# A one-core perceiver layer: where the first eight attention steps do their splits, loads and seeding

## What is computed

```python
def xattn(inputs_q, inputs_kv, Wq, Wk, Wv, Wo):        # H, HD = 16, 128
    q = (inputs_q @ Wq).reshape(b, sq, H, HD) * (1.0 / np.sqrt(HD))
    k = (inputs_kv @ Wk).reshape(b, skv, H, HD)
    v = (inputs_kv @ Wv).reshape(b, skv, H, HD)
    attn = softmax(einsum('bqhd,bkhd->bhqk', q, k), axis=-1)
    return einsum('bhqk,bkhd->bqhd', attn, v).reshape(b, sq, H * HD) @ Wo

x = x + xattn(layernorm(x), ctx, Wq, Wk, Wv, Wo)       # 1 x 128 x 512 against 1 x 12544 x 512
x = x + decayed_linear_attention(layernorm(x), ...)    # 16 heads of 32
x = x + bitlinear_ffn(layernorm(x), ...)               # 512 -> 2048 -> 512
```

## Time and profile before

| | |
|---|---|
| median of 3 runs | 2038.02 us (2037.34 to 2038.19) |
| the profiled execution: its own time | 2039.78 us |
| its span | 2037.9 us |
| PE busy | 1955.8 us (96%) |
| DVE busy | 1606.4 us (79%) |
| ACT busy | 1127.4 us (55%) |

### The profile page before, as it was taken

How to read it: one execution, slowest core, us unless ns; L and a number is a source line. 1 busy time by engine, 2 the same in 40 slices (tenths; PEclk the granted TensorE clock), 3 DMA queues, 4 the chain that set the end, 5 groups by cost and what they waited for, 6 DMA issues and landing times.

```text
span 2037.9 us, 46247 instructions
## 1 busy us (share of the span) xinstructions
PE 1955.8 (96%) x17334; PEld 1596.3 (78%) x17334; DVE 1606.4 (79%) x3444; ACT 1127.4 (55%) x2484; POOL 272.4 (13%) x465
## 2 busy tenths in 40 slices
PE   5799999999999999999999999999999999999786
PEld 5577887887887987977978978878878878878462
DVE  4788788788888888888888888888888887877426
ACT  3556566666656555555555565555565556555212
POOL 1011111111111111111111111111111111100001
PEclk8899999999999999999999999999999999999888
DMA  5568887887886888787787887888978877765540
GB/s 147 148 113 163 164 162 153 160 165 153 163 161 133 143 161 162 145 160 156 146 165 156 147 156 156 147 155 162 168 147 157 147 136 142 138 121 128 206 177 6
DMA packets 966945, 304.44 MB, mean 149 GB/s; under 512 B 893985, under 2 KB 952865, under 8 KB 965825
## 3 DMA queue, kind: packets, MB, share of 16 engines
q1 hardware_dynamic: 966720, 301.47, 74.8%
HBM read 72.16 MB, written 4.46 MB: 38 GB/s over the span
## 4 chain that ended last, share of the span: by engine, by line
PE 91%; DVE 5%; DMA 2%; issue 1%; ACT 1%; POOL 0%; DVEq 0%; ACTq 0%; SPq 0%; POOLq 0%
PE ps_v L1211 25%; PE ps_s L1196 24%; PE ps_t L1196 19%; PE ps_w L1211 18%; DMA bulk<-in_vo 1%; PE ps_w L1170 1%; DVE pp L875 1%; PE ps_v L1183 1%; PE ps_t L1290 1%; DVE acc L884 0%; PE ps_s L1333 0%; PE ps_v L1297 0%; DVE prob L870 0%; ACT bulk L602 0%; PE ps_s L1152 0%
## 5 line engine op out<-in xcount | busy, mean ns | idle before, releaser
L1196 PE MATMUL ps_s<-bulk 128*128 128x128 f16 (+2 forms) x4752 | 583.4, 272 | 2.7 <-DVE bulk L811 2.7
L1211 PE MATMUL ps_v<-nring,pt 128*128 128x256 f16 x4704 | 581.4, 273 | 3.0 <-DVE acc L884 1.5
L1211 PEld LDWEIGHTS ps_v<-nring,pt 128*128 128x128 f16 x4704 | 458.8, 98 | 63.7 <-DVE acc L794 2.6
L1196 PEld LDWEIGHTS ps_s<-bulk 128*128 128x128 f16 x4752 | 404.6, 98 | 114.7 <-DVE bulk L811 2.9
L1196 PE MATMUL ps_t<-bulk 128*128 128x384 f16 (+2 forms) x3564 | 454.0, 272 | 18.9 <-ACT ps_t L653 17.2
L1211 PE MATMUL ps_w<-nring,pt 128*128 128x256 f16 x3528 | 451.8, 273 | 8.0 <-DVE ps_w L894 6.4
L875 DVE SCALAR_TENSOR_TENSOR pp<-prob,pp 128x384 f16<-128x384 f32 (+4 forms) x680 | 423.5, 689 | 0.0
L1196 PEld LDWEIGHTS ps_t<-bulk 128*128 128x128 f16 x3564 | 301.8, 98 | 111.6 <-ACT ps_t L653 18.9
L1211 PEld LDWEIGHTS ps_w<-nring,pt 128*128 128x128 f16 x3528 | 340.0, 98 | 57.5 <-DVE ps_w L894 8.6
L633 ACT ACTIVATE pp<-prob 128x384 f16<-128x384 f32 (+4 forms) x680 | 370.9, 623 | 5.5 <-DVE prob L870 4.7
L622 ACT ACTIVATE prob<-ps_s,nmax 128x768 f32<-128x768 f32 (+2 forms) x136 | 119.1, 876 | 431.6 <-DVE nmax L850 424.9
(11 more groups left out here) (187 smaller groups left out, 1410.5 us busy)
## 6 DMA issues: line engine op xcount, KB each, us to landing
stage<-in_ctx SPq DMA_DIRECT2D x196, 128.0 KB, 2.9
wst<-in_w SPq DMA_DIRECT2D x64, 256.0 KB, 3.2
bulk<-in_vo SPq DMA_DIRECT2D x16, 512.0 KB, 6.4
acc<-in_qk SPq DMA_DIRECT2D x11, 512.0 KB, 4.1
pt<-pp SPq DMA_TRANSPOSE x272, 5.6
tern_d<-wter SPq DMA_DIRECT2D x32, 128.0 KB, 2.9
bulk<-tern_d SPq DMA_DIRECT2D x2, 2048.0 KB, 11.1
nring<-in_aw SPq DMA_DIRECT2D x3, 1024.0 KB, 8.4
```

The source lines that it names most:

```text
L1196: ins = mm(out if n == 1 else out.rearrange("p (n m) -> p n m", m=P), q_part(e, qlo, a)[:, c * P:(c + 1) * P], t_moving(k, run, tlo, b, c) ...
L1211: ins = mm(dst, pt[:, tile:tile + P], n_part(c, clo, b), start=(first and n == 0 and plo == 0 and clo == 0), stop=(last and n == w - 1 and ...
```

## The change

- `split_hi` and `q_hi_part` move on ACT, in steps 0 to 7, from the end of a step to a place behind the copy `part_u` of the next (`q_hi_part(k+1)` there, `split_hi(k)` behind `q_copy`). `q_lo_part(k+1)` moves on DVE from the end of the step before to a place behind the first maximum; the first piece of `split_lo` from the step's start to a place ahead of the first sum of the probabilities.
- Ahead of the loop `q_hi_part(0)` and `q_lo_part(0)` move up, and those of pair 1 into step 0.
- The q/k weights get a fourth slot, which serves head 3 alone. Heads 0 to 6 are loaded ahead of block 1 of the context, heads 7 and 8 behind the first `turn_n`, and in the loop two more (2k+7, 2k+8) behind `load_ctx` rather than ahead of it.
- The two banks are seeded by eight bf16 matmuls of the identity with itself, 128 columns each, as soon as the bf16 identity is there; the transposed queries go through `ps_s`.
- In steps 0 to 4 the last value product is put off: it follows the first score product of the step that comes next.

```diff
@@ -167,9 +167,13 @@
             at = (h + 4) % H * D
             return acc[:, at:at + D]
 
+        def qk_place(i):
+
+            return (i, 1) if i < 4 else ((i - 4) % 3, (i - 4) // 3 + 2)
+
         def qk_slot(i):
 
-            return (acc[:, 0:2 * D], wst[:, :], acc[:, 6 * D:8 * D])[i % 3]
+            return (acc[:, 0:2 * D], wst[:, :], acc[:, 6 * D:8 * D], acc[:, 14 * D:16 * D])[qk_place(i)[0]]
 
         def q32(ii):
             return prob[:, 0:8 * BLK] if ii == 1 else acc[:, 2 * D:6 * D]
@@ -256,7 +260,7 @@
 
         in_x = sem("in_x")
         in_const = sem("in_const")
-        in_qk = [sem(f"in_qk{k}") for k in range(3)]
+        in_qk = [sem(f"in_qk{k}") for k in range(4)]
         in_vo = [sem(f"in_vo{k}") for k in range(4)]
         in_ctx = sem("in_ctx")
         in_nt = [sem(f"in_nt{g}") for g in range(2)]
@@ -415,9 +419,9 @@
         @block.sync
         def _(sp):
             def load_qk(g):
-                if g >= 3:
-                    sp.wait_ge(qk_mm, g - 2)
-                sp.dma_start(qk_slot(g), qk_d[Q_ORDER[g]]).then_inc(in_qk[g % 3], 16)
+                if g >= 4:
+                    sp.wait_ge(qk_mm, g - 3 if g < 7 else g - 2)
+                sp.dma_start(qk_slot(g), qk_d[Q_ORDER[g]]).then_inc(in_qk[qk_place(g)[0]], 16)
 
             def load_ctx(c):
                 if c:
@@ -447,11 +451,10 @@
             load_qk(0)
             load_qk(1)
             load_ctx(0)
-            for g in range(2, 6):
+            for g in range(2, 7):
                 load_qk(g)
             load_ctx(1)
-            load_qk(6)
-            load_qk(7)
+
             def load_w(n):
                 if n >= 2 * WP + 2:
                     sp.wait_ge(w_quant, n - 2 * WP - 1)
@@ -469,15 +472,14 @@
                 sp.dma_start(ring_vo[:, (f % 4) * SL:(f % 4 + 1) * SL], vo_d[Q_ORDER[f]]).then_inc(in_vo[f % 4], 16)
 
             turn_n(0)
+            load_qk(7)
+            load_qk(8)
             for k in range(1, NS + 1):
                 turn_p(k - 1, 0)
                 turn_p(k - 1, 1)
                 for c in range(1, NCH):
                     if SPLIT_AT[c] == k - 2:
                         turn_n(c)
-                for g in (2 * k + 6, 2 * k + 7):
-                    if g < H:
-                        load_qk(g)
                 if k == NS - 2:
                     sp.wait_ge(s4_done, max(i for i, step in enumerate(STEPS) if step[0] == 5) + 1)
                     for f in range(4):
@@ -491,6 +493,9 @@
                 for c in range(2, NCH):
                     if SPLIT_AT[c] == k + 2:
                         load_ctx(c)
+                for g in (2 * k + 7, 2 * k + 8):
+                    if g < H:
+                        load_qk(g)
             sp.wait_ge(s4_done, NS)
             sp.wait_ge(in_pt[1], 16 * NS)
             sp.dma_start(diff[:, :], diff_d).then_inc(in_const, 16)
@@ -583,7 +588,7 @@
         @block.scalar
         def _(act):
             act.wait_ge(ytp, 1)
-            nc.scalar.activation(xt[:, :], ps_t[:, 0:D], ACT.Copy).then_inc(ytc, 1)
+            nc.scalar.activation(xt[:, :], ps_s[:, 0:D], ACT.Copy).then_inc(ytc, 1)
 
             def q_copy(ii):
                 act.wait_ge(q_mm, ii + 1)
@@ -657,8 +662,12 @@
                 nc.scalar.activation(part_e[:, 0:cols(k)], bank_e(k), ACT.Copy).then_inc(e_copied, 1)
                 act.wait_ge(s6_done, k + 1)
                 nc.scalar.activation(part_u[:, 0:cols(k)], bank_b(k), ACT.Copy).then_inc(u_copied, 1)
+                if k + 1 < NP:
+                    q_hi_part(k + 1)
                 if ii < NP:
                     q_copy(ii)
+                if k < NP:
+                    split_hi(k)
                 if 0 <= k - ABS_AT < 2 * WP:
                     n = k - ABS_AT
                     piece = wst[:, (n % 2) * D:(n % 2 + 1) * D]
@@ -681,17 +690,15 @@
                     for g, h in enumerate(heads_of(k)):
                         last = nc.scalar.activation(alpha[:, h:h + 1], nmax_of(k, g, 1), ACT.Exp, bias=nmax_of(k, g), scale=-1.0)
                     last.then_inc(al_done, 1)
-                if ii < NP:
-                    q_hi_part(ii)
-                split_hi(k + 1)
+                if k + 1 >= NP:
+                    split_hi(k + 1)
 
             q_copy(0)
             q_out(0)
             split_hi(-1)
+            q_hi_part(0)
             q_copy(1)
-            q_hi_part(0)
             q_out(1)
-            q_hi_part(1)
             for k in range(NS):
                 step(k)
 
@@ -917,10 +924,12 @@
                     nc.vector.tensor_scalar(wter[:, (n % 2) * D:(n % 2 + 1) * D], piece, -1.0, None, ALU.max).then_inc(w_quant, 1)
 
             def step(k):
-                if k:
+                if k >= NP:
                     split_lo(k, 0)
                 v.wait_ge(s2_done, k + 1)
                 max_head(k, 0)
+                if k + 1 < NP:
+                    q_lo_part(k + 1)
                 v.wait_ge(s7_done, k + 1)
                 v.wait_ge(e_copied, k + 1)
                 add_and_max(k, 1)
@@ -934,6 +943,8 @@
                 if k + 2 < NP:
                     q_out(k + 2)
                     q_four_sums(k + 2)
+                if k < NP:
+                    split_lo(k, 0)
                 if k == ABS_AT + 2 * WP + 1:
                     v.wait_ge(w_abs, 2 * WP)
                     nc.vector.tensor_reduce(wsc[:, 0:2], wabs[:, :].rearrange("p (m n) -> p m n", m=2), AX.X,
@@ -956,8 +967,6 @@
                 lo_part(k, S3, 1, 3)
                 lo_part(k, S2, 1, 4)
                 lo_part(k, S4, 1, 5)
-                if k + 2 < NP:
-                    q_lo_part(k + 2)
                 if k == NP - 2:
                     v.wait_ge(q_lo, NP)
                 if k >= LAG:
@@ -970,10 +979,9 @@
             q_four_sums(0)
             for n in range(3):
                 split_lo(-1, n)
+            q_lo_part(0)
             q_out(1)
-            q_lo_part(0)
             q_four_sums(1)
-            q_lo_part(1)
             for k in range(NS):
                 step(k)
             v.wait_ge(lo_done, 5 * NS)
@@ -1153,11 +1161,13 @@
                 return last
 
 
+            pe.wait_ge(dve, 1)
+            for bank in (ps_t[:, 0:D], ps_b):
+                for c in range(KC):
+                    mm(bank[:, c * P:(c + 1) * P], identb[:, :], identb[:, :], start=(c == 0), stop=(c == KC - 1), skip_group_check=True)
             pe.wait_ge(ydone, 1)
-            transposes(ps_t, y0, KC, ident).then_inc(ytp, 1)
+            transposes(ps_s, y0, KC, ident).then_inc(ytp, 1)
             pe.wait_ge(ytc, 1)
-            for bank in (ps_t[:, 0:D], ps_b):
-                mm(bank, ident[:, :], xt[:, :], start=True, stop=True, skip_group_check=True)
 
             def q_heads(ii):
 
@@ -1165,7 +1175,7 @@
                     pe.wait_ge(acc_done[0], ii - 4)
                 for i in (2 * ii, 2 * ii + 1):
                     w = qk_slot(i)
-                    pe.wait_ge(in_qk[i % 3], 16 * (i // 3 + 1))
+                    pe.wait_ge(in_qk[qk_place(i)[0]], 16 * qk_place(i)[1])
                     for c in range(KC):
                         last = mm(ps_c[:, BLK + (i % 2) * HD:BLK + (i % 2 + 1) * HD], w[:, c * HD:(c + 1) * HD], xt[:, c * P:(c + 1) * P],
                                   start=(c == 0), stop=(c == KC - 1), skip_group_check=True)
@@ -1234,6 +1244,14 @@
                 value_product(k, val_b, S3, T1, False, False).then_inc(v7_done, 1)
                 pe.wait_ge(ve_copied, k + 1)
                 value_product(k, val_e, S4, B11, False, True).then_inc(v3_done, 1)
+                if not put_off(k):
+                    last_value(k)
+
+            def put_off(k):
+
+                return k < NP and STEPS[k][2] < WIN
+
+            def last_value(k):
                 pe.wait_ge(vd_done, k + 1)
                 value_product(k, val_b, V22, T4, False, True).then_inc(v4_done, 1)
 
@@ -1246,6 +1264,8 @@
                 pe.wait_ge(ctx_lo, 3 * (a + w))
                 ii = k + 2
                 product(k, bank_a(k), A11, B11, True, False).then_inc(s1_done, 1)
+                if k > LAG and put_off(k - LAG - 1):
+                    last_value(k - LAG - 1)
                 product(k, bank_e(k), S1, T1, True, False).then_inc(s5_done, 1)
                 pe.wait_ge(a_copied, k + 1)
                 product(k, bank_b(k), S2, T2, False, False).then_inc(s6_done, 1)
```

## The result

The changed kernel takes 2029.46 us (median of 5, 2026.59 to 2031.08) against 2038.02 us: a ratio of 0.9956, 95% interval 0.9942 to 0.9971, so 8.6 us faster where 10.7 was forecast. Its profiled execution took 2030.27 us with a span of 2028.5. The two spans differ by 9.4 us, and the first A product of step 8, from which PE is full, has moved from 148.58 to 139.43 us: 9.15 of the 9.4 lie ahead of it.

A forecast was written before the change was run, and what follows sets the result against it. PE bounds the kernel, with 40.8 us idle to save; carried gains of 7.0, 10.1, 10.8, 6.0, 8.5, 9.4, 11.2, then + 2.1 - 1.9 - 0.7, give 10.7 us: 2027.3 us against the median, range 2021.5 to 2033.5.

The forecast's parts named there:

- the opening: Start to step 0's copy L653: shorter seeding, earlier head 3 and moved parts bring it 7.9 us earlier, 7.0 carried.
- the skill's rule on the clock: First `q_heads`: array throttled until active, so its 2.0 us would double, leaving 1.3 of the seeding's 3.3 us; not adopted.
- Steps 0 to 1 and 1 to 2: Copies ending steps 0 and 1: L602 and L611 no longer ahead, 3.1 us; then net 0.7 us; carried 10.8.
- The stall at head 9: Step 2: `q_heads(4)` waits 3.8 us for head 9, loaded behind context block 2; range 2.6 to 3.8 us.
- Its clock price: Step 2, behind the wait for head 9: eight fp32 matmuls and two products at half speed, 1.0 us.
- Steps 3 to 5: `q_heads` of steps 3 to 5: shorter waits for copy, `value_sum_d` and accumulators; carried 8.5, 9.4, 11.2 us.
- Steps 5 to 7: Step 5's end gains 2.1 us; step 6's sum loses 1.9; split piece and later lo parts cost 0.7.
- (a): Step 2: no stall at head 9; gain 15.5 us, 2022.5 us, or 2020.8 if the clock stays up; chance 0.2.
- (b): Steps 0 to 7: DVE becomes the bound, `q_lo_part` ahead of two sums; gain 5 us, 2033 us; chance 0.12.
- (c): Steps 3 to 6: gaps keep the clock at 0.50; 26 us lost, 15 us slower net, 2053 us; chance 0.03.
- (d): Loads: another than head 9 is late, such as head 7; 2030 us; chance 0.1 with others.
- The signs: Expected in the trace: waits for L653 under 8 us, step 0 at 19.7, `in_qk` wait over 2, PE full from about 129.

The follow-up runs named there:

- e2: The changed kernel with 22 added bf16 identity matmuls in PE's opening waits (18 for the layer norm, 4 for `xt`): 2025.87 us.
- e3: The changed kernel with the old fp32 seeding of 512 columns behind `xt`: 2030.63 us.
- e1: The changed kernel with the loads of heads 2k+7 and 2k+8 ahead of the context block's load again, as before the change: 2021.36 us.
- e8: The changed kernel with three q/k slots and all q/k and context loads in the old order: 2021.46 us.
- e7: e1 with all three `split_lo` pieces behind the sums of the probabilities and `value_sum_d`, in steps 1, 3 and 6: 2024.26 us.
- e6: e5 with more bf16 identity matmuls in PE's long waits (pair 1 primes, copies of steps 1 and 2, `value_sum_d` of step 4): 2020.72 us.
- e5: The changed kernel with the edits of both e1 and e2: 2019.12 us.
- e9: The changed kernel with old loads, old fp32 seeding and no put-off, leaving only the moves on ACT and DVE: 2027.93 us.
- e11: The changed kernel timed once more, with no edit: 2028.16 us.

## Why the prediction was right, and where it was not

The sign and the mechanism held: PE was full behind step 8, the time saved ahead of it was kept, and the largest loss was the load of head 9. The size held in part by luck: against the numbers carried, the opening brought 2.1 us less and step 2 another 1.1 less, and steps 3 to 7 gave 1.6 us of it back. Step by step, how much earlier a point is reached:

| point | forecast | measured | from |
|---|---|---|---|
| copy of step 0 | 7.9, carried 7.0 | 4.9 | 28.57 to 23.67 |
| copy of step 1 | 10.1 | 8.0 | 42.84 to 34.84 |
| copy of step 2 | 10.8 | 8.7 | 57.61 to 48.90 |
| end of step 2, first value product | 6.0 | 2.9 | 65.68 to 62.82 |
| q_heads of step 3 | 8.5 | 5.4 | 75.00 to 69.63 |
| q_heads of step 4 | 9.4 | 6.3 | 92.06 to 85.73 |
| q_heads of step 5 | 11.2 | 8.4 | 107.92 to 99.55 |
| step 8 | 10.7 | 9.15 | 148.58 to 139.43 |

**The opening** is the term that failed: 4.9 instead of 7.9 us. The prediction set the skill's rule on the clock against the window's 1.00 at the start and let the window decide. e2 and e3 show that the rule was right. The row at 0 us was no measurement: PE had done nothing there that could show a clock, and the length of the matmuls, which does, was in the trace. Two lines of the kernel before, to set beside the earlier trace rows:

```profile
10.54 1.58 PE L1160 MATMUL ps_w<-acc,ident 128*128 128x512 f32 x2
12.85 1.06 PE L1170 MATMUL ps_w<-acc,wst 128*128 128x128 f32 x8
```

The first two fp32 matmuls of 512 columns took 0.94 us each (8.67 to 10.54), the other two 0.70 (to 11.95); right behind them eight of 128 columns took 0.11 us each (11.95 to 12.85), so that 512 columns at that speed take 0.45. The 1.3 us that the prediction gave "by the rule" is what the end of the first `q_heads` shows (13.9 to 12.5): 1.9 us less than forecast. The primes of pair 1, slow again behind a wait of 2.66 us, took another 1.0 us. Nor was it DVE that set the start of step 0, as the prediction has it: `q_lo_part(0)` was done at 21.88 us (L818, 19.86 plus 2.02), and step 0 started at 22.78 right behind the primes.

**Steps 0 to 1 and 1 to 2**: 3.1 and 0.7 forecast, 3.1 and 0.7 measured. `q_hi_part` and `q_lo_part` hid as forecast, and `split_lo` ahead of the sums took its 0.95 us.

**The stall at head 9**: forecast 3.8, measured 3.93, at the place and for the reason given; the load landed 4.8 us after its issue where 4.6 were taken. Its clock price was put at 1.0 us, and 1.9 is what the table of steps leaves (8.7 less 3.93 less 2.9); e1 gives 1.8. This term was sized too low.

**Steps 3 to 5** gained 2.5, 1.0 and 2.0 us where 2.5, 0.9 and 1.8 were forecast. **Steps 5 to 7**: L602 and L611 gave 2.4 (forecast 2.1), the sum of step 6 lost 1.7 (forecast 1.9; PE waits 1.79), and the 0.7 us for the split piece and late lo parts didn't come: PE's wait for `value_sum_d` in step 7 is 0.36 us, and was 0.57 before.

**The rivals.** (a) fell by the 3.9 us row, but its price, 15.5 us, was the right order: e1 and e8 gave 17 by the medians, 16.2 and 15.2 at step 8. (b) is half true: DVE binds steps 3, 4 and 6, as e7 and e6 show, though not by `q_lo_part` in every step. (c) the clock did cost more than I carried, yet about 2.8 us over the whole lead-in and not 26. Its premise, that the clock fell after every gap of 2.5 us and more, doesn't hold in every run: behind a wait of 2.75 us in step 4 the next six matmuls of 256 columns took 1.40 us in the changed kernel and 0.82, full speed, in e1, e5 and e8. (d) no other load was late.

**The signs.** Most of what was to show it did: the first `q_heads` starts at 8.75 us, PE waits 3.93 us for `in_qk` with head 9 issued behind four `stage` loads, and 1.79 us for the sum L841 (the old L834) in step 6, and it's full from 125.8 us on (about 129 forecast). Two signs failed: the waits for the copy fell to 8.4 us and not to under 8, and step 0 starts at 22.78 and not at 19.7. The second is the opening again.

## What to carry to other kernels

Moving late-needed work from in front of a copy that PE waits for to a place behind it paid what was forecast here, step by step, and could be costed from the old trace to 0.3 us. A load must be placed by the last wait ahead of it in its queue, not by its own: one transfer behind another's semaphore cost all that the seeding and the put-off gained. And a stall is priced with the matmuls behind it: where they ran at half speed (behind the 3.9 us at head 9), its removal gave back 5.7 us, about one and a half times its length, and shortening two waits by making a third one longer (3.46 us in e7) lost.

## What was not expected of the hardware

- The granted clock shown for the opening (1.00) is not the clock that the matmuls ran at: eight fp32 matmuls of 128 columns took 2.07 us at 8.75 us and 1.06 us at 14.42 us. The window over the first of the two (the granted clock is the third number from the end):

```profile
8.00:10.00 2.00, 1.31 (x7) 1.25 (x7) 0.00 (x0) 0.60 (x1) 0.82 (x2) 1.00 1.03 391
```

- Runs of one kernel differ by up to 10 us (2033.2 to 2043.4 for the kernel before, beside e9 to e11; 2023.9 to 2031.2 in e11); up to step 8 the two executions of the changed kernel in the traces have the same idle time and 1.4 us of difference in busy time.
- DVE was slowed while POOL worked. In e7, DVE's fp32 sums of 256 columns, 0.42 us elsewhere, took 0.92 and 0.94 us while POOL's L551 ran from 54.12 us:

```profile
54.12 3.20 POOL L551 TENSOR_TENSOR stage<-stage 128x256 f32<-128x256 f32 x4 [21.98 <-DMA stage<-in_ctx]
```
```profile
55.81 0.92 DVE L809 TENSOR_TENSOR acc<-acc 128x256 f32<-128x256 f32 x1
56.66 0.94 DVE L810 TENSOR_TENSOR acc<-acc 128x256 f32<-128x256 f32 x1
57.53 0.41 DVE L812 TENSOR_TENSOR acc<-acc 128x256 f32<-128x256 f32 x1
```

The Trainium skill (Trainium Architecture — The Big Picture, What this means for kernel authors) says that VectorE and GpSimd contend for a shared port pair, and that it is an exclusive lock, not a split; the rows agree for operations with two inputs in SBUF. A change that starts a block's sums at another time moves this collision with it, here by 1 us of DVE.
